# Cross-attention scores in two 64-row strips of the array, keys replicated through device memory, stages unrolled

## The chip, the cores and the metric

The kernel runs on one core of one Trainium2 chip. The metric is the device time of one execution in microseconds, the median of several runs. TensorE is called PE here, VectorE DVE, ScalarE ACT, GpSimd POOL, and SyncE (which issues all DMAs of this kernel) SP.

## What is computed

Four attention layers run one after the other on a small query block `x` (8 batches, 100 rows, width 128) against a long context `ctx` (8 batches, 1444 rows, width 128). All have 16 heads of 8 elements. Layers 0, 1 and 3 attend to the whole context. Layer 2 attends to its first 100 rows under a causal mask and has a feed-forward part.

```python
q, k, v = x @ Wq + bq, ctx @ Wk + bk, ctx @ Wv + bv     # 16 heads of 8
scores = einsum('bhqd,bhkd->bhqk', q, k) / sqrt(8)      # 16 x 100 x 1444 for each batch
attn = softmax(scores, axis=-1)
out = einsum('bhqk,bhkd->bhqd', attn, v)                # then projection, residual, norm
# layer 1: score = where(mask, -inf, score); the mask is all False in these inputs
```

## The kernel before

**Units and stages.** A unit is one batch of layer 0, 1 or 3: 24 units. Five steps of different units run side by side in a stage: `load` reads the context of a unit, `prep` transposes it and makes keys and queries, `top` makes the scores for the row maximum and the values, `exp` makes the scores again, takes the exponential and multiplies by the values, `post` normalises and projects. A unit moves on by one step per stage, so there are 24 stages with an `exp` unit, three ahead of them and one behind. Layer 2 of a batch rides along in the stages where layer 3 is loaded and prepared.

**Steps.** A stage has 48 steps (`NSTEP`): 12 chunks of 120 or 121 context rows, by 4 groups `t` of 4 heads. At step j every engine runs its part of `exp` tile j, and what the tables `AT` and `AT2` place at j: the transposes `ct0..2`, keys `k0..2`, queries `q`, values `v0..2`, and so on. Each of these is a few matmuls into one of two PSUM banks (`shared`), read by ACT or DVE. All engines run their instructions in the order in which they are written, and wait on semaphores whose names say what they count (`probs_ready` k: ACT has made k tiles of exponentials).

**A score tile.** Keys and queries are each split into two float16 parts, and the product is the sum of three: high by high, high by low, low by high. These three stand below each other in the rows of the array: 3 parts by 32 (4 heads of 8) are 96 rows (`PARTS`). The stationary operand is a piece of `krep` (96 rows, 120 context rows as columns), the moving operand `qmax` (96 rows, 4 heads by 100 queries = 400 columns, with zeros where the row is of another head). For `exp` the tile is `qexp`, a copy of `qmax` with a 97th row that holds minus the maximum, against a row of ones in `krep`. So at each step PE runs one matmul of 400 columns into one of two banks `sexp` (it waits until ACT has read the tile before the last), then one or two of 400 columns into one of three banks `smax`, which DVE folds into `mx`:

```python
MAX_AT = [i * 39 // NSTEP for i in range(NSTEP)]   # 48 maximum tiles in steps 0 to 38
def exp_scores(u, j, masks):      # PE, L700
    pe.wait_ge(*at(pe, "probs_ready", u, j - SR + 1))                      # SR = 2
    pe.matmul(ps, krep[:, u.par, t, c0:c0 + r], qexp[:, u.par, t, :, :]...)
def max_scores(u, j, masks):      # PE, L664
    pe.wait_ge(*at(pe, "smax_used", u, j - MR + 1))                        # MR = 3
    pe.matmul(ps, krep[0:PARTS, u.par, t, c0:c0 + r], qmax[:, u.par, t, :, :]...)
```

**Behind the scores.** ACT turns `sexp` into `probs` (L965). Every fourth step PE multiplies four tiles of `probs` by `vx` into `acc` (L719, 8 float32 matmuls, recorded as 16; each uses a strip of 32 columns of the array, four strips at a time). At step 39, when DVE has folded all 48 tiles, PE transposes `mx` into the banks `smax` (L676), DVE takes the maximum (`mneg`, L1102), PE transposes it at step 42 (L684), ACT copies it (`mrow`), and a DMA puts it into row 97 of `qexp` for the next stage.

**Keys.** ACT and POOL make `kp` (128 rows: 4 groups of 32; high and low part). `replicate` (SP, L403) spreads it into `krep` with 12 DMAs for each of the three groups of chunks, 36 a unit, of 30 KB each. ACT may overwrite `kp` for the next unit when these have landed.

**Loops.** `pipeline` writes most stages out, but stages 1 to 4, 9 to 12 and 17 to 20 as a hardware loop of two passes over two stages, whose semaphore counts stand in registers (`at`, L266). On PE, a branch on a flag computed from the mask stands ahead of stage 7: the variant of stages 7 to 15 that adds the mask is not taken with these inputs.

Of the kernel before, what the change touches and what calls it, by code (L numbers as in the profile page):

```python
# [21 lines left out]
F32 = mybir.dt.float32  # L22
# [9 lines left out]
KEYS = 1444  # L32
# [15 lines left out]
PARTS = 3 * 32  # L48
# [17 lines left out]
      "v0": 22, "v1": 24, "v2": 26, "mk0": 28, "mk1": 30, "mk2": 32, "mn": 42}  # L66
# [6 lines left out]
        "v1": 0, "v2": 1, "mk0": 0, "mk1": 1, "mk2": 0, "mn": 1, "flag": 1}  # L73
# [3 lines left out]
         "pt22": 1, "pt23": 0, "o2": 1, "mn": 0}  # L77
TOGETHER = 4
VALUES_AT = [j // TOGETHER * TOGETHER + TOGETHER + 1 for j in range(NSTEP)]
MAX_AT = [i * 39 // NSTEP for i in range(NSTEP)]  # L80
MT_AT = 39
# [3 lines left out]
class Unit:  # L85

    def __init__(self, layer, batch, reg=None, parity=None):
        self.L, self.batch, self.reg = layer, batch, reg
        self.par = batch % 2 if parity is None else parity

    def rows_of(self, tile):

        if self.reg is None:
            return tile[:, self.batch, :]
        return tile[:, bass.ds(self.reg + self.batch if self.batch else self.reg, 1), :].rearrange("s a d -> s (a d)")


def build(nc, ctx_in, x_in, mask_in, w_qkv, w_o, w_1, w_2, rows_in, cols_in, bq_in, headmask_in, heads_in, ident_in,
          causal_in, out):
    with ExitStack() as es:  # L100
# [3 lines left out]
        def psum(name, banks=1):  # L104
# [16 lines left out]
        headmask = sb("headmask", [PARTS, HT])  # L121
        headmask16 = sb("headmask16", [PARTS, HT], F16)
# [30 lines left out]
        krep = sb("krep", [PARTS + 1, 2, T, KEYS], F16)  # L153
# [5 lines left out]
        qmax = sb("qmax", [PARTS, 2, T, HT, S], F16)  # L159
        qexp = sb("qexp", [PARTS + 1, 2, T, HT, S], F16)  # L160
        mx = sb("mx", [128, T * QW], F16)
# [31 lines left out]

        smax = [psum(f"smax{i}") for i in range(MR)]
# [12 lines left out]
            "q_parts": one, "q_spread": one, "qexp_in": [16, 16, 0, 16], "v_filled": G, "v_ready": G,  # L207
# [3 lines left out]
            "m_ready": [2, 2, 0, 2], "mn_filled": one, "mrow_ready": one, "mrow_in": [16, 16, 0, 16],  # L211
# [9 lines left out]
        for g in range(3):  # L221
            PER[f"krep_in{g}"] = [16 * 12 * bool(n) for n in NG]

        for name, per in {"nat2_in": 32, "cx2_filled": 1, "cx2_read": 1, "kqv2_filled": 1, "kqv2_read": 1,
# [10 lines left out]
                "OT": ("oT_ready", 1), "wo": ("wo_read", 1), "cx2": ("cx2_read", 1), "kqv2": ("kqv2_read", 1),  # L235
# [10 lines left out]
        registers = {}  # L246

        def at(engine, name, u, k):


            per = PER[name][u.L]
            value = B * sum(PER[name][:u.L]) + per * u.batch + k
            if u.reg is None or not per:
                return sem[name], max(value, 0)
# [8 lines left out]
            if value == 0:  # L263
                return sem[name], term
# [1052 lines left out]
```

## Time and profile before

| | |
|---|---|
| time, median of 3 runs | 1240.93 us (1237.69 to 1241.09) |
| time of the profiled execution | 1242.44 us |
| its span, first to last instruction | 1240.6 us |
| mean granted clock of PE | 0.959 |
| busy: PE, DVE, ACT, POOL | 85%, 69%, 67%, 30% of the span |
| ahead of the first `exp` tile | 91.2 us |
| stages 0 to 7 (layer 0) | 357.9 us |
| `exp` stage 5; 17 (with layer 2); 23 (`exp` alone) | 40.8; 52.1; 30.4 us |

A matmul is recorded from its start until its modelled end, some 0.17 us after its last column has entered, so a busy PE isn't a full PE. "Idle before" is the time an engine stood still ahead of an instruction, with what ended it.

### The profile page before, as it was taken

How to read it: one execution, taken by the hardware profiler on the slowest of the kernel's cores; microseconds unless marked ns; L12 is line 12 of the kernel's file. 1: busy time of each engine (PE TensorE's matmuls, PEld its weight loads, DVE VectorE, ACT ScalarE, POOL GpSimd, SP SyncE). 2: the span in 40 equal slices, each digit the busy share in tenths (PEclk: the TensorE clock that was granted, in tenths of full speed). 3: DMA queues.
4: the chain of work that ended last, by engine and by line, in shares of the span. 5: the costliest groups of instructions: out<-in, count | busy, mean ns of one | idle time of the engine just before them, and what ended most of it. 6: DMA issues, size and time to landing. Idle time of an engine off the chain costs nothing.

```text
span 1240.6 us, 30123 instructions
## 1 busy us (share of the span) xinstructions
PE 1059.6 (85%) x9938; PEld 638.9 (51%) x9938; DVE 857.3 (69%) x1757; ACT 825.3 (67%) x1788; POOL 372.6 (30%) x339
## 2 busy tenths in 40 slices
PE   1469888888998999988998889998999989998886
PEld 0245445445555555655555555565556556565442
DVE  5678678578766766875876657576777858777650
ACT  1237756667776777776777676657677766767565
POOL 6744433344411311330231413232242413323000
PEclk9979999899999999998999999799999999999898
DMA  7212212212221221221232120202021121201100
GB/s 187 62 37 58 61 27 58 58 30 60 65 58 33 73 74 32 72 79 38 58 77 52 39 71 21 55 24 58 22 62 35 48 61 28 61 24 31 35 3 4
DMA packets 57587, 62.92 MB, mean 51 GB/s; under 512 B 16826, under 2 KB 50906, under 8 KB 57302
## 3 DMA queue, kind: packets, MB, share of 16 engines
q1 hardware_dynamic: 57430, 60.89, 19.0%
q8 instruction: 91, 1.49, 0.5%
q14 instruction: 66, 0.54, 0.1%
HBM read 23.63 MB, written 0.41 MB: 19 GB/s over the span
## 4 chain that ended last, share of the span: by engine, by line
PE 58%; DVE 16%; issue 10%; ACT 10%; SPq 3%; DMA 1%; POOL 1%; DVEq 0%; ACTq 0%; POOLq 0%
PE sexp L700 15%; PE acc L719 14%; PE smax L664 12%; DVE mx L1096 7%; ACT probs L965 5%; PE shared L616 3%; PE shared L604 3%; SPq L403 2%; DVE mneg L1102 2%; PE shared L593 2%; PE shared L784 2%; PE smax L676 1%; DVE qs L1083 1%; PE shared L626 1%; SPq L469 1%
## 5 line engine op out<-in xcount | busy, mean ns | idle before, releaser
L965 ACT ACTIVATE probs<-sexp 120x400 f32<-120x400 f32 (+1 forms) x1152 | 558.9, 511 | 237.9 <-PE sexp L700 226.6
L1096 DVE TENSOR_TENSOR mx<-smax,mx 120x400 f16<-120x400 f32 (+1 forms) x1056 | 557.2, 567 | 167.7 <-PE smax L664 161.4
L700 PE MATMUL sexp<-qexp,krep 97*120 97x400 f16 (+1 forms) x1152 | 403.8, 360 | 61.1 <-ACT probs L965 41.8
L664 PE MATMUL smax<-qmax,krep 96*120 96x400 f16 (+1 forms) x1152 | 367.3, 350 | 37.5 <-DVE mx L1096 29.1
L700 PEld LDWEIGHTS sexp<-qexp,krep 97*120 97x120 f16 (+1 forms) x1152 | 152.1, 136 | 216.7 <-ACT probs L965 144.6
L719 PE MATMUL acc<-probs,vx 120*18 120x200 f32 (+1 forms) x4608 | 262.1, 347 | 1.0 <-ACT probs L965 0.9
L664 PEld LDWEIGHTS smax<-qmax,krep 96*120 96x120 f16 (+1 forms) x1152 | 157.6, 138 | 92.6 <-DVE mx L1096 51.3
L488 POOL TENSOR_TENSOR ct<-ctf,ct 128x480 f16<-128x480 f32 (+1 forms) x72 | 82.8, 1151 | 346.2 <-ACT ct L902 346.2
L719 PEld LDWEIGHTS acc<-probs,vx 120*18 120x18 f32 (+1 forms) x4608 | 109.0, 99 | 114.8 <-issue 84.5
L1094 DVE CAST mx<-smax 121x400 f16<-121x400 f32 x96 | 51.3, 570 | 120.3 <-PE smax L664 120.2
L488 POOL TENSOR_TENSOR kp<-kf,kp 128x480 f16<-128x480 f32 (+1 forms) x72 | 79.2, 1106 | 114.6 <-ACT kp L916 114.6
L516 POOL TENSOR_TENSOR qmax<-qs,headmask 96x400 f16<-96x400 f16 x96 | 79.0, 852 | 52.9 <-DVE qs L1084 52.9
L494 POOL TENSOR_TENSOR rstd<-vare,half 100x1 f32<-100x1 f32 x24 | 13.0, 542 | 223.1 <-DVE vare L1113 223.1
L927 ACT COPY vx<-shared 120x512 f32<-120x512 f32 (+1 forms) x72 | 42.4, 589 | 50.7 <-PE shared L616 50.7
L604 PE MATMUL shared<-ct,wk 128*128 128x480 f16 (+1 forms) x216 | 60.4, 391 | 14.9 <-ACT kp L916 4.8
L593 PE MATMUL shared<-ident,nat 120*128 120x120 f32 (+1 forms) x288 | 46.9, 291 | 27.0 <-DMA causal<-in_causal 20.5
L1102 DVE TENSOR_REDUCE mneg<-smax 100x8 f16<-100x968 f16 x48 | 53.7, 1160 | 17.8 <-PE smax L676 17.8
L616 PEld LDWEIGHTS shared<-wv,ct 128*120 128x120 f16 (+1 forms) x864 | 62.1, 139 | 6.0 <-DVE sc L1166 1.8
L616 PE MATMUL shared<-wv,ct 128*120 128x128 f16 (+1 forms) x864 | 63.1, 225 | 1.1 <-DVE sc L1166 1.1
L593 PEld LDWEIGHTS shared<-ident,nat 120*128 120x128 f32 (+1 forms) x288 | 39.1, 156 | 34.1 <-DMA causal<-in_causal 20.5
L916 ACT ACTIVATE kf<-shared,cols 128x480 f32<-128x480 f32 (+1 forms) x48 | 32.0, 666 | 16.3 <-PE shared L604 15.1
L604 PEld LDWEIGHTS shared<-ct,wk 128*128 128x128 f16 x216 | 17.5, 99 | 43.3 <-issue 26.2
(133 smaller groups left out, 994.0 us busy)
## 6 DMA issues: line engine op xcount, KB each, us to landing
nat<-in_ctx SPq DMA_DIRECT2D x24, 720.0 KB
krep<-kp SPq DMA_DIRECT2D x576, 30.0 KB, 1.9
krep<-kp SPq DMA_DIRECT2D x288, 30.2 KB, 1.9
qexp<-qmax SPq DMA_DIRECT2D x24, 300.0 KB, 3.4
maskexp<-maskmax SPq DMA_DIRECT2D x8, 281.2 KB, 3.4
anymask<-in_mask SPq DMA_DIRECT2D x1, 1128.1 KB, 6.7
mask<-in_mask SPq DMA_DIRECT2D x8, 141.0 KB
wq<-in_w_qkv SPq DMA_DIRECT2D x1, 768.0 KB
```

The source lines that it names most:

```text
L488: pool.tensor_tensor(dst[:, 1, c0:c0 + n], src[:, c0:c0 + n], dst[:, 0, c0:c0 + n], ALU.subtract).then_inc(sem[done], 1)
L516: last = pool.tensor_tensor(qmax[:, u.par, t, :, :], qs[:, t, :].unsqueeze(1).broadcast_to([PARTS, HT, S]), headmask16[:, :].unsqueeze(2). ...
L593: last = pe.transpose(ps[:, to:to + r], nat[0:r, c, :], ident[0:r, 0:r])
L604: last = pe.matmul(ps[:, 0:n], wk16[:, w, u.L, :], ct[:, u.par, c, c0:c0 + n], start=(j == 0), stop=(j == 2))
L616: last = pe.matmul(ps[0:r, D * i:D * i + D], ct[:, u.par, p, c0:c0 + r], wv16[:, w, u.L, :], start=(j == 0), stop=(j == 2))
L664: last = pe.matmul(ps, krep[0:PARTS, u.par, t, c0:c0 + r], qmax[:, u.par, t, :, :].rearrange("p h s -> p (h s)"), start=True, stop=not masks)
L700: last = pe.matmul(ps, krep[:, u.par, t, c0:c0 + r], qexp[:, u.par, t, :, :].rearrange("p h s -> p (h s)"), start=True, stop=not masks)
L719: last = pe.matmul(acc[32 * q:32 * q + VW, 2 * S * slot:2 * S * slot + 2 * S], vx[0:r, u.par, PAIRS * c + 2 * t + p, :], probs[0:r, j % PR ...
L965: act.activation(probs[0:r, j % PR, :], sexp[j % SR][0:r, 0:QW], ACT.Exp).then_inc(sem["probs_ready"], 1)
L1094: op = dve.tensor_copy(dst, src)
L1096: op = dve.tensor_tensor(dst, src, dst, ALU.max)
L1102: dve.tensor_reduce(mneg[:, 8 * i:8 * i + 8], smax[i][0:S, :].bitcast(F16).rearrange("s (h n) -> s h n", h=8)[:, :, 0:chunk(0)[1]], AX, AL ...
```

## The change

Score products use half of the array's rows. A strip of 64 rows holds 2 heads: 3 parts by 16 rows (`KROWS` = 48), then a row for the maximum. Heads 4t and 4t+1 stand in the upper strip (rows 0 to 63), 4t+2 and 4t+3 in the lower one, so that one query tile `qx` (128 rows, 2 heads by 100 = 200 columns for each t) holds all four. Both uses read it: the maximum products rows 0 to 47 of a strip, the `exp` products 49 rows. It has three buffers; `qexp` and its DMA are gone. A tile of 400 columns is now one strip of two t, two matmuls of 200 columns each. The tile for `exp` and the tile for the maximum are taken in turn, and since `LEAD` is odd they always lie in different strips and different banks.

The 48 maximum tiles are spread one to a step, and run 13 tiles ahead (`LEAD`): the first 13 of a unit fall into steps 35 to 47 of the stage before. `mx` has two buffers, and its transposes go to the `shared` banks, at steps 36 and 37; `mn` is at 41.

Keys go to device memory first (`kept`, 3 DMAs a unit) and are read back into `krep` with 6 DMAs a group instead of 12, each 16 rows by 4 t. ACT may overwrite `kp` when the 3 writes have landed. All stages are written out, without loops or register counts.

```diff
-PARTS = 3 * 32
+PARTS = 128
+STRIP = 64
+KROWS = 48
-MAX_AT = [i * 39 // NSTEP for i in range(NSTEP)]
-MT_AT = 39
+LEAD = 13
+        kept = nc.dram_tensor("kept", (2, 128, 2, KEYS), F16, kind="Internal").ap()
-        def at(engine, name, u, k):
...
+        def at(name, u, k):
+
+            return sem[name], max(B * sum(PER[name][:u.L]) + PER[name][u.L] * u.batch + k, 0)
+        def tile_of(j):
+
+            return j // T, j // 2 % 2, j % 2
+        def max_tile(s, j):
+
+            u, i = (s.top, j + LEAD) if j + LEAD < NSTEP else (s.prep, j + LEAD - NSTEP)
+            return (u, i) if u is not None else None
-                b0 = units[n].batch if 0 <= n < len(units) else None
-                if b0 == 1 and n + 3 <= last:
...
-                    with engine.Fori(1, 4, 2) as b:
...
+                run(stage_of(n, units), n)
+                n += 1
-                for t in range(T):
+                for i in range(2):
                     for j, part in enumerate((0, 0, 1)):
-                        sp.dma_start(krep[32 * j:32 * j + 32, u.par, t, c0:c0 + n],
-                                     kp[32 * t:32 * t + 32, part, c0:c0 + n]).then_inc(sem[f"krep_in{g}"], 16)
+                        at_row = STRIP * i + 16 * j
+                        sp.dma_start(krep[at_row:at_row + 16, u.par, :, c0:c0 + n],
+                                     kept[u.par, :, part, c0:c0 + n].rearrange("(t i r) n -> i r t n", t=T, i=2)[i]
+                                     ).then_inc(sem[f"krep_in{g}"], 16)
+            def max_product(u, j, a, masks):
...
+                    pe.wait_ge(*at("smax_used", u, j - MR + 1))
+                at_row = STRIP * i
+                ps = smax[j % MR][0:r, 0:QW]
+                last = pe.matmul(ps[:, 2 * S * a:2 * S * a + 2 * S], krep[at_row:at_row + KROWS, u.par, 2 * tp + a, c0:c0 + r],
+                                 qx[at_row:at_row + KROWS, u.third, 2 * tp + a, :, :].rearrange("p f s -> p (f s)"),
...
+            def exp_product(u, j, a, masks):
...
+                    pe.wait_ge(*at("probs_ready", u, j - SR + 1))
+                at_row = STRIP * i
+                ps = sexp[j % SR][0:r, 0:QW]
...
-                    if s.exp is not None:
-                        exp_scores(s.exp, j, masks and s.exp.L == 1)
-                    for i in range(NSTEP):
-                        if MAX_AT[i] == j and s.top is not None:
-                            max_scores(s.top, i, masks and s.top.L == 1)
+                    m = max_tile(s, j)
+                    for a in range(2):
+                        if s.exp is not None:
+                            exp_product(s.exp, j, a, masks and s.exp.L == 1)
+                        if m is not None:
+                            max_product(*m, a, masks and m[0].L == 1)
```

The same place of PE's program before and after, in a stage of layer 0 around step 24, where `v1` lies. Before, steps 23 to 25; `sexp` and `smax` are score banks, `shared` the values, `acc` the products with the values:

```order
L700 MATMUL sexp1<-qexp,krep 120x400 [waits probs_ready]
L664 MATMUL smax2<-qmax,krep 120x400 [waits smax_used]
L700 MATMUL sexp0<-qexp,krep 120x400 [waits probs_ready]
L664 MATMUL smax0<-qmax,krep 120x400 [waits smax_used]
L616 MATMUL shared0<-wv16,ct 120x128 [waits q_read]
L616 MATMUL shared0<-wv16,ct 120x128 x11
L700 MATMUL sexp1<-qexp,krep 120x400 [waits probs_ready]
L664 MATMUL smax1<-qmax,krep 120x400 [waits smax_used]
L719 MATMUL acc<-probs,vx 18x200 x8
```

After, steps 24 and 25:

```order
L661 MATMUL sexp0<-qx,krep 120x200 [waits probs_ready]
L622 MATMUL smax1<-qx,krep 120x200 [waits smax_used]
L661 MATMUL sexp0<-qx,krep 120x200
L622 MATMUL smax1<-qx,krep 120x200
L572 MATMUL shared0<-wv16,ct 120x128 [waits q_read]
L572 MATMUL shared0<-wv16,ct 120x128 x11
L661 MATMUL sexp1<-qx,krep 120x200 [waits probs_ready]
L622 MATMUL smax2<-qx,krep 120x200 [waits smax_used]
L661 MATMUL sexp1<-qx,krep 120x200
L622 MATMUL smax2<-qx,krep 120x200
L683 MATMUL acc<-probs,vx 18x200 x8
```

Each pair of 400 columns became four of 200 that alternate; the second half of an `exp` tile now stands behind the wait for `smax_used`.

The end of a stage on PE, where the maxima are transposed (`mx`, then `mneg`). Before:

```order
L664 MATMUL smax2<-qmax,krep 120x400 [waits smax_used]
L700 MATMUL sexp1<-qexp,krep 120x400 [waits probs_ready]
L676 MATMUL smax0<-ident16,mx 100x121 [waits smax_used]
L676 MATMUL smax0<-ident16,mx 100x121 x7
L676 MATMUL smax1<-ident16,mx 100x121 x8
L700 MATMUL sexp0<-qexp,krep 120x400 [waits probs_ready]
L700 MATMUL sexp1<-qexp,krep 120x400 [waits probs_ready]
L719 MATMUL acc<-probs,vx 18x200 x8
L700 MATMUL sexp0<-qexp,krep 120x400 [waits probs_ready]
L684 MATMUL shared1<-ident16,mneg 16x100 [waits mask_ready,m_ready]
```

After:

```order
L661 MATMUL sexp0<-qx,krep 120x200 [waits probs_ready]
L622 MATMUL smax1<-qx,krep 121x200 [waits smax_used]
L661 MATMUL sexp0<-qx,krep 120x200
L622 MATMUL smax1<-qx,krep 121x200
L638 MATMUL shared1<-ident16,mx 100x121 [waits v_ready,smax_used]
L638 MATMUL shared1<-ident16,mx 100x121 x7
L661 MATMUL sexp1<-qx,krep 120x200 [waits probs_ready]
L622 MATMUL smax2<-qx,krep 121x200 [waits smax_used]
L661 MATMUL sexp1<-qx,krep 120x200
L622 MATMUL smax2<-qx,krep 121x200
L683 MATMUL acc<-probs,vx 18x200 x8
L638 MATMUL shared0<-ident16,mx 100x121 [waits v_ready,smax_used]
```

The transposes moved from `smax` to the `shared` banks, and the next unit's maximum tiles (121 rows: its first chunk) run on around them.

## Rows read from the trace of the kernel before

**Rows 1.** The page: the span, and busy time by engine.
```profile
span 1240.6 us, 30123 instructions
PE 1059.6 (85%) x9938; PEld 638.9 (51%) x9938; DVE 857.3 (69%) x1757; ACT 825.3 (67%) x1788; POOL 372.6 (30%) x339
```

**Rows 2.** The page: the chain that ended last, by engine.
```profile
PE 58%; DVE 16%; issue 10%; ACT 10%; SPq 3%; DMA 1%; POOL 1%; DVEq 0%; ACTq 0%; POOLq 0%
```

**Rows 3.** Stages 14, 5, 17 and 23: length, busy time by engine, PEclk, DMA share, GB/s.
```profile
728.50:787.20 58.70, 53.45 (x470) 32.72 (x469) 39.18 (x86) 38.32 (x84) 16.58 (x14) 0.89 0.17 45
318.40:359.20 40.80, 37.72 (x383) 22.17 (x382) 29.86 (x60) 30.70 (x68) 9.90 (x10) 1.00 0.22 55
899.40:951.50 52.10, 48.10 (x467) 30.49 (x467) 39.26 (x85) 37.72 (x84) 16.57 (x14) 1.00 0.18 46
1201.00:1231.40 30.40, 24.52 (x243) 10.14 (x242) 2.90 (x13) 21.79 (x49) 0.54 (x1) 1.00 0.01 3
```

**Rows 4.** Groups by line: busy us, mean ns, idle before.
```profile
L965 ACT ACTIVATE probs<-sexp 120x400 f32<-120x400 f32 (+1 forms) x1152 | 558.9, 511 | 237.9 <-PE sexp L700 226.6 <-issue 4.1
L1096 DVE TENSOR_TENSOR mx<-smax,mx 120x400 f16<-120x400 f32 (+1 forms) x1056 | 557.2, 567 | 167.7 <-PE smax L664 161.4
```

**Rows 5.** PE in order of time, steps 20 to 24 of stage 11: start, length.
```profile
602.84 0.50 PE L664 MATMUL smax<-qmax,krep 96*120 96x400 f16 x2
603.27 0.88 PE L719 MATMUL acc<-probs,vx 120*18 120x200 f32 x16
604.08 0.38 PE L700 MATMUL sexp<-qexp,krep 97*120 97x400 f16 x1
...
605.05 0.84 PE L616 MATMUL shared<-wv,ct 128*121 128x128 f16 x12
605.72 0.33 PE L700 MATMUL sexp<-qexp,krep 97*120 97x400 f16 x1
605.90 0.33 PE L664 MATMUL smax<-qmax,krep 96*120 96x400 f16 x1
606.07 0.33 PE L700 MATMUL sexp<-qexp,krep 97*120 97x400 f16 x1
```

**Rows 6.** ACT in order of time, late in stage 5, with maximum tiles.
```profile
346.00 2.05 ACT L965 ACTIVATE probs<-sexp 120x400 f32<-120x400 f32 x4 [0.78 <-PE sexp L700]
348.83 2.05 ACT L965 ACTIVATE probs<-sexp 120x400 f32<-120x400 f32 x4 [0.79 <-PE sexp L700]
```

**Rows 7.** ACT in order of time in stage 23, without maximum tiles.
```profile
1210.20 1.93 ACT L965 ACTIVATE probs<-sexp 121x400 f32<-121x400 f32 x4 [0.32 <-PE sexp L700]
1212.75 1.94 ACT L965 ACTIVATE probs<-sexp 120x400 f32<-120x400 f32 x4 [0.61 <-PE sexp L700]
```

**Rows 8.** The chain of stages 0 to 7 (91.2 to 449.1 us), by line.
```profile
by line: PE sexp L700 18.6%; PE acc L719 16.7%; PE smax L664 16.7%; issue 6.9%; DVE mx L1096 6.7%; PE shared L616 4.9%; ACT probs L965 4.9%; PE shared L604 4.6%; DVE mneg L1102 3.7%; PE shared L593 3.3%; DVE qs L1083 2.6%; DVE ssq L1063 1.6
```

**Rows 9.** Waits of the whole span: us in total, times, longest.
```profile
PEld smax L664 <- DVE mx L1096: 51.3, 82, 3.4
PEld smax L676 <- DVE mx L1096: 14.2, 16, 1.3
PEld shared L684 <- DVE mneg L1102: 6.6, 8, 1.7
```

**Rows 10.** PE's weight loads in order of time: behind two of four such gaps.
```profile
229.16 0.18 PEld L700 LDWEIGHTS sexp<-qexp,krep 97*121 97x121 f16 x1 [3.47 <-issue]
1005.85 0.13 PEld L700 LDWEIGHTS sexp<-qexp,krep 97*121 97x121 f16 x1 [3.51 <-issue]
```

**Rows 11.** The stretch around the first of them, columns as in rows 3.
```profile
228.10:234.70 6.60, 5.53 (x29) 3.20 (x30) 2.01 (x4) 2.67 (x6) 1.10 (x1) 0.50 0.18 46
```

**Rows 12.** PE in order of time: the first maximum tile.
```profile
44.86 0.92 PE L664 MATMUL smax<-qmax,krep 96*121 96x400 f16 x2 [6.53 <-POOL qmax L516]
```

**Rows 13.** The chain before stage 0: first key DMA's issue, last one's landing.
```profile
34.95 0.63 SPq L403
57.17 1.82 DMA krep<-kp
```

More of the change, by code:

```diff
@@ L320, in build @@
         held = [None, None]
-        def last_uses(s):
-            ends = [(AT["v1"], "v1", s.top), (AT["mk2"], "mk2", s.prep if s.prep.L == 1 else None),
-                    (AT["mn"], "mn", s.top), (AT2["o"], "o2", s.att2)]
-            for _, use, u in sorted((x for x in ends if x[2] is not None), key=lambda x: x[0]):
-                held[bank(use, u)] = (use, u)
         def await_read(pe, i):
@@ L393, in replicate @@
             def replicate(u, g, before, steps):
                 _, c0, n, _ = groups()[g]
-                counts = [at(sp, "k_lo", u, g + 1)]
+                sp.wait_ge(*at(f"k_kept{g}", u, 16))
                 if before is not None:
-                    counts.append(at(sp, "sexp_ready", before, steps))
-                for count in counts:
-                    sp.wait_ge(*count)
-                for t in range(T):
+                    sp.wait_ge(*at("sexp_ready", before, steps))
+                if u is UNITS[0] and g == 0:
+                    sp.wait_ge(sem["ones_ready"], 2)
@@ L869, in stage @@
                         queries(s.prep)
-                    if s.top is not None and j == MT_AT:
-                        maxima(s.top)
+                    for i in range(2):
+                        if s.top is not None and j == AT[f"mt{i}"]:
+                            maxima(s.top, i)
                     if s.top is not None and j == AT["mn"]:
@@ L1207, in stage @@
                 for j in range(NSTEP):
-                    for i in range(NSTEP):
-                        if MAX_AT[i] == j and s.top is not None:
-                            maximum(s.top, i)
+                    m = max_tile(s, j)
+                    if m is not None:
+                        maximum(*m)
                     if s.post is not None and j == AT["O"] + 1:
@@ L1226, in stage @@
                             power(s.load, part)
-                    if s.top is not None and j == MT_AT:
-                        for i in range(2):
+                    for i in range(2):
+                        if s.top is not None and j == AT[f"mt{i}"]:
                             maxima(s.top, i)
@@ L1272, in _ @@
             dve.memset(ones[:, :], 1.0).then_inc(sem["rest_ready"], 1)
[L1273 removed]
+            pipeline(UNITS, stage, first=-2)
 def kernel(**inputs):
```

447 lines of the change are left out of this document (204 added, 243 removed).

## Prediction

> **What bounds the kernel now.** I read the page first. No engine is full: PE is recorded busy for 85% of the span, DVE for 69%, ACT for 67%, POOL for 30% [rows 1]. PE's share is of matmuls whose recorded ends overlap, so the chain says more: it runs through PE for 58%, through DVE for 16%, through ACT for 10% [rows 2]. The table by stage shows the same balance in a stage without layer 2: 40.8 us long, ACT busy 30.7, DVE 29.9 [rows 3]. Neither could carry the stage alone, and a stage could not be much shorter than 31 us however fast PE was.
>
> PE in order of time gives the true price of its work. With nothing to wait for, score matmuls of 400 columns start 0.17 us apart (605.72, 605.90, 606.07), and twelve matmuls of 128 columns with as many weight loads start (0.84 - 0.22) / 11 = 0.056 us apart [rows 5]. A group of `acc` takes from 603.27 to 604.08. The two score tiles of each of 48 steps are thus 48 x 0.34 = 16.3 us of each stage, its largest item.
>
> How much of that stands on the path is seen in two ways. Bare steps, without preparation: four tiles of exponentials take 348.83 - 346.00 = 2.83 us with maximum tiles beside them [rows 6], and 1212.75 - 1210.20 = 2.55 us in the last stage, which has none [rows 7]. So four maximum tiles, 0.68 us of PE, cost 0.28 us there. ACT's four tiles are 1.94 us of this; the rest is the wait behind `acc`. In steps with preparation PE is the tighter one: the chain of the eight stages of layer 0 runs through L664 for 16.7% of 357.9 us, 59.8 us, or 7.5 us a stage [rows 8].
>
> **The change, part by part.**
>
> *Two strips side by side.* A step has four matmuls of 200 columns in place of two of 400. If the strips work at once, a step's scores take 0.17 us instead of 0.34, 8.2 us less PE time a stage. Of this the path gives back between 0.28 x 39/4 = 2.7 us (maximum tiles now stand in 39 of 48 steps, all priced as bare) and 7.5 us (all of L664 on the chain). Both kinds of step fill a stage about equally, so I take the middle, 5.1 us, for the 23 stages that have maximum tiles: **-118** (bounds -62 and -172). ACT's and DVE's tiles keep their shapes and counts (511 and 567 ns each [rows 4]).
>
> The trace has no two row strips at work, but it has four column strips: the 16 `acc` records start within 0.88 - 0.33 = 0.55 us, 0.037 us apart for 200 float32 columns, where the 400-column float16 ones need 0.17 [rows 5]. That makes overlap likely for rows too. The Trainium skill, "TensorE: Matmul & The Clock Gate", part 3, says that matmuls in different row groups run concurrently, starting about 4 ns apart; the trace before cannot confirm that.
>
> *Weight loads.* There are four of 120 columns a step instead of two. At 0.056 us each one behind the other they are 0.22 us, more than the 0.17 of the matmuls. If they don't overlap between strips, a stage gains 0.05 x 48 = 2.4 us less; with PE's 58% of the path that is +32 over 23 stages. I take 0 and keep it for the range.
>
> *Turns between modes.* Score tiles now use 64-row strips, the preparation the whole array, `acc` column strips. The trace has the last turn: the score matmul at 602.84 + 0.50 - 0.33 = 603.01 has let in its columns by 603.18, and `acc` starts at 603.27: 0.09 us. The way back: the last `acc` matmul starts at 603.82, is in by 603.99, and `sexp` starts at 604.08, 0.09 again [rows 5]. Between scores and preparation there was nothing: 605.72 follows the values at matmul pace. There are 17 such places in a stage of layer 0, 4 of them behind `acc` already, so 30 new turns; 36 with the mask's transposes; some 56 with layer 2. In all (30 + 36 + 56) x 8 = 976 turns, 88 us of PE. After a turn to the preparation ACT or DVE waits for its result; the turn back lies under their copy of it. I take half: **+44** (bounds 0 and +88). The Trainium skill, "TensorEngine Tiling (Array Packing)", Key Properties, says that changing the tiling mode drains the engine; this speaks against the change, and the 0.09 us above agrees with it. By the rule all 976 turns would count, +88.
>
> *Maxima.* Before, PE stopped at step 39 for DVE's last tile, and at 42 for `mneg`: 14.2 and 6.6 us in all [rows 9]. With the last tile at step 34, transposes at 36 and 37 into other banks and `mn` at 41, other tiles lie between: **-21**. The work itself is the same.
>
> *Loops.* Four gaps of PE of 3.5 to 3.9 us are put down to "issue" at a stage's start; those at 229.16 and 1005.85 are back edges [rows 10], and so is one at 580.78. They go: **-11**. The fourth, at 404.05, is the branch on the mask flag, and stays, one stage earlier. Stages that are already written out show no such gap, so I cost the longer program at 0.
>
> *Keys.* SP's issues of 0.63 us [rows 13], 36 a unit, are 22.7 us; now there are 18 with twice the pieces, and 3 writes. In the loop of stages the copy may begin at exp step 16 and is needed at step 35, some 16 us later, against six issues of perhaps 1 us and two landings of 1.8 [rows 13]: hidden. If it weren't, PE would stop at step 35. Before stage 0 it matters: ACT waited for the last landing at 57.17 + 1.82 = 59.0 before the next unit's keys, and maximum tiles, which began at 44.86 [rows 12], were then held behind the next unit's transposes. Thirteen of them now come first: **-5**.
>
> *Queries.* POOL spreads half the columns, and one copy by DMA goes; DVE's split of the queries works on 128 rows instead of 96 with as many columns. All this has steps to spare, priced at 0.
>
> *A new wait.* The second half of an `exp` tile stands behind the maximum's wait for DVE. Behind it are ACT's next tile and `acc`. PE waited there 51.3 us in 82 waits [rows 9]; ACT has one more tile to work on, (2.05 - 0.51) / 3 = 0.51 us at most and 0.45 at its best, so some 51.3 - 82 x 0.45 = **+14** get through (bounds 0 and +51).
>
> The sum: -118 + 44 - 21 - 11 - 5 + 14 = -97. The profiled execution took 1242.4 us, its span 1240.6 plus 1.8 around it, and lies 1.5 above the median of the runs. 1242.4 - 97 - 1.5 = **1144 us**.
>
> **The rivals.**
>
> - *PE drops off the path.* The gain is -172, the turns cost nothing, the new wait 14: 1242 - 172 - 21 - 16 + 14 = 1047 at best, 1080 with part of the turns. For it: 7.5 us on L664's chain. Against: ACT's chain is close behind in bare steps. Chance 0.15.
> - *Turns and loads eat the gain.* Lower bound of the gain, all turns, serial loads: -62 + 88 + 32 - 21 - 16 + 14 = +35; with half of the loads and three quarters of the turns, 1240. It needs PE to be the tight engine at the turns but not in the scores, which [rows 6] and [rows 7] allow for bare steps only. As a band of 1200 to 1245: chance 0.16.
> - *The strips don't overlap* (the change doesn't do what it says). Scores keep 0.34 us a step, and the turns are paid three quarters: 0 + 66 - 21 - 16 + 14 = +43, 1284. Slower. Against it are the column strips in [rows 5]. Chance 0.09.
> - *The clock falls.* PE is granted half speed in stretches behind its gaps: 0.50 from 228.1 to 234.7, around the gap that ends at 229.16 [rows 10, 11]. Stage 14 at a mean of 0.89 took 58.7 us where stage 17, with the same work and a clock of 1.00, took 52.1 [rows 3]: 6.6 us for 0.11 x 58.7 x 2 = 12.9 us at half speed, 0.51 per us. PE's array now has 8 us less work in each stage, and might be judged idle oftener. The gain of 97 is gone at 190 us more of half speed, a mean clock of 0.88 instead of 0.96; at 0.80 the kernel takes some 1320. Slower. Chance 0.10.
> - *Late keys* through device memory, or other waits that leave no change: chance 0.03.
>
> The forecast itself has 0.47, with a range of its own from 1090 to 1200.
>
> **How the numbers follow.** From the forecast and the first rival the time lies from 1050 to 1200 with 0.62; the range reaches up over the second rival to 1240 and down to 1065, and leaves out the two slower ones. About 0.3%, 4 us, is what a measurement of this kernel can tell from no change. Faster: 0.47 + 0.15 + 0.13 of the second rival = 0.75; within 0.3%: 0.04; slower: 0.09 + 0.10 + 0.02 = 0.21.
>
> **What would show it.** Strips: in the new trace score matmuls of neighbouring steps start in pairs a few ns apart, four of them in 0.17 us. Weight loads: L661 and L622 loads starting closer than 0.05 us. Turns: 0.09 us of idle array on both sides of each preparation. Bare steps: four tiles of ACT in 2.55 to 2.65 us. Maxima: no wait of L638 for DVE. Loops: one gap of over 3 us on PE, not four. New wait: ACT's waits for L661 that end with DVE's tile. I'd be wrong if the pairs start 0.08 us apart or more, if the mean clock is under 0.9, or if ACT's wait for `sexp` (226.6 us [rows 4]) grows.

## The result

The changed kernel takes **1310.5 us** (median of four runs, 1297.1 to 1319.5) against 1241.0 (1237.7 to 1242.7) of the kernel before, run beside it: 1.053 times as long, 95% interval 1.045 to 1.061. It is slower; 1144 was forecast. Medians here and below are of all runs of a kernel, and ratios leave out a run that is over 1.5% above its kernel's shortest, here the one of 1319.5.

The page of the profile after, which answers to [rows 1] and [rows 2], with the granted clock in 40 slices:

```profile
span 1309.2 us, 30985 instructions
PE 1144.4 (87%) x12242; PEld 671.1 (51%) x12242; DVE 868.2 (66%) x1758; ACT 831.9 (64%) x1788; POOL 339.9 (26%) x339
PEclk9999977877978788889687779887788977779675
PE 63%; DVE 13%; ACT 12%; issue 8%; SPq 1%; DMA 1%; POOL 1%; ACTq 0%; POOLq 0%; DVEq 0%
```

PE is recorded busier than before and its share of the chain grew from 58% to 63%. The mean granted clock is 0.829 in place of 0.959. PE is granted one of two clocks, 2.4 or 1.2 GHz. A mean of 0.829 thus says that 1309.2 x (1 - 0.829) x 2 = 448 us of the span were at 1.2, against 102 before.

Stages 4, 14, 17 and 23 after, in the columns of [rows 3]:

```profile
274.00:325.30 51.30, 46.72 (x480) 26.36 (x480) 33.64 (x64) 31.21 (x68) 16.91 (x16) 0.70 0.21 52
762.20:820.30 58.10, 52.08 (x566) 31.03 (x567) 39.59 (x87) 38.59 (x85) 15.22 (x14) 0.88 0.20 53
940.10:997.90 57.80, 55.31 (x563) 32.80 (x564) 39.00 (x86) 38.76 (x84) 15.29 (x14) 0.80 0.19 49
1257.80:1299.90 42.10, 34.68 (x290) 15.70 (x289) 2.89 (x13) 21.87 (x49) 0.54 (x1) 0.53 0.01 3
```

Stage 17 had the full clock before and took 52.1 us; now it has 0.80 and takes 57.8. Stage 23, which has no maximum tiles and no preparation, went from 30.4 us at 1.00 to 42.1 at 0.53. DVE's and ACT's own work is the same size. Their waits for PE grew instead (groups as in [rows 4]):

```profile
L1062 DVE TENSOR_TENSOR mx<-smax,mx 120x400 f16<-120x400 f32 (+1 forms) x1056 | 570.7, 570 | 324.9 <-PE smax L622 319.4
L931 ACT ACTIVATE probs<-sexp 120x400 f32<-120x400 f32 (+1 forms) x1152 | 556.5, 512 | 307.7 <-PE sexp L661 295.9
```

ACT waited 295.9 us for `sexp` (226.6 before), DVE 319.4 for `smax` (161.4).

Yet the mechanism itself works. PE in order of time, at full clock in stage 11 (columns as in [rows 5]):

```profile
608.80 0.29 PE L661 MATMUL sexp<-qx,krep 49*121 49x200 f16 x1
608.80 0.29 PE L622 MATMUL smax<-qx,krep 48*120 48x200 f16 x1
608.93 0.25 PE L661 MATMUL sexp<-qx,krep 49*121 49x200 f16 x1
608.94 0.25 PE L622 MATMUL smax<-qx,krep 48*120 48x200 f16 x1
609.11 0.88 PE L683 MATMUL acc<-probs,vx 121*18 121x200 f32 x16
609.92 0.29 PE L661 MATMUL sexp<-qx,krep 49*121 49x200 f16 x1
```

The two strips start in the same hundredth of a microsecond. Bare steps are what was forecast, too: ACT's four tiles at the end of stage 11 take 641.22 - 638.67 = 2.55 us (2.83 in [rows 6]):

```profile
638.67 1.93 ACT L931 ACTIVATE probs<-sexp 120x400 f32<-120x400 f32 x4
641.22 0.90 ACT L931 ACTIVATE probs<-sexp 120x400 f32<-120x400 f32 x2 [0.61 <-PE sexp L661]
```

Of the four gaps of PE of over 3 us one is left, the branch on the mask flag:

```profile
367.73 0.18 PEld L661 LDWEIGHTS sexp<-qx,krep 49*121 49x121 f16 x1 [3.82 <-issue]
```

So the question is which of two theories holds. **Clock**: half-empty columns of the array, 48 or 49 rows of 128, bring the clock down, and that alone is the loss. **Turns**: the turns between tiling modes and the doubled loads eat the gain and more, and the clock only follows the gaps that they make.

### The profile page after: what moved, and what is told of

Read it like the earlier page. It is cut to its first block, busy times and chain, and to the rows that moved or that the text cites. A ratio compares the mean times of both kernels' runs of the same rounds, so it can differ in the third digit from the quotient of the medians.

```text
span 1309.2 us, 30985 instructions
## 1 busy us (share of the span) xinstructions
PE 1144.4 (87%) x12242; PEld 671.1 (51%) x12242; DVE 868.2 (66%) x1758; ACT 831.9 (64%) x1788; POOL 339.9 (26%) x339
## 4 chain that ended last, share of the span: by engine, by line
PE 63%; DVE 13%; ACT 12%; issue 8%; SPq 1%; DMA 1%; POOL 1%; ACTq 0%; POOLq 0%; DVEq 0%
PE sexp L661 18%; PE acc L683 17%; ACT probs L931 7%; DVE mx L1062 4%; PE smax L622 4%; PE shared L560 4%; PE shared L549 4%; PE shared L572 3%; PE shared L638 3%; PE shared L748 2%; ACT kp L882 2%; PE shared L582 2%; PE shared L738 1%; DVE qs L1049 1%; PE shared L729 1%
## 5 line engine op out<-in xcount | busy, mean ns | idle before, releaser
L1062 DVE TENSOR_TENSOR mx<-smax,mx 120x400 f16<-120x400 f32 (+1 forms) x1056 | 570.7, 570 | 324.9 <-PE smax L622 319.4
L931 ACT ACTIVATE probs<-sexp 120x400 f32<-120x400 f32 (+1 forms) x1152 | 556.5, 512 | 307.7 <-PE sexp L661 295.9
L661 PE MATMUL sexp<-qx,krep 49*120 49x200 f16 (+1 forms) x2304 | 454.5, 303 | 74.2 <-ACT probs L931 67.0
L622 PE MATMUL smax<-qx,krep 48*120 48x200 f16 (+1 forms) x2304 | 450.7, 304 | 20.3 <-DVE mx L1062 12.3
L661 PEld LDWEIGHTS sexp<-qx,krep 49*120 49x120 f16 (+1 forms) x2304 | 245.1, 150 | 304.0 <-ACT probs L931 187.6
L683 PE MATMUL acc<-probs,vx 120*18 120x200 f32 (+1 forms) x4608 | 317.5, 404 | 1.7 <-ACT probs L931 1.0
L622 PEld LDWEIGHTS smax<-qx,krep 48*120 48x120 f16 (+1 forms) x2304 | 242.5, 152 | 39.7 <-DVE mx L1062 27.5
L549 PE MATMUL shared<-ident,nat 120*128 120x120 f32 (+1 forms) x288 | 63.3, 362 | 23.4 <-POOL nat L492 21.5
L1068 DVE TENSOR_REDUCE mneg<-shared 100x8 f16<-100x968 f16 x48 | 55.9, 1164 | 22.6 <-PE shared L638 22.6
L472 POOL TENSOR_TENSOR qx<-qs,headmask 128x200 f16<-128x200 f16 x96 | 47.1, 522 | 53.6 <-DVE qs L1050 53.6
L638 PE MATMUL shared<-ident,mx 121*100 121x121 f16 x384 | 40.0, 266 | 1.0
```

Of the source, the lines that this page charges most:

```text
L549: last = pe.transpose(ps[:, to:to + r], nat[0:r, c, :], ident[0:r, 0:r])
L622: last = pe.matmul(ps[:, 2 * S * a:2 * S * a + 2 * S], krep[at_row:at_row + KROWS, u.par, 2 * tp + a, c0:c0 + r], qx[at_row:at_row + KROWS ...
L638: last = pe.transpose(ps[0:S, :].bitcast(F16)[:, 128 * h:128 * h + n], mx[0:n, u.par, col:col + S], ident16[0:n, 0:n])
L661: last = pe.matmul(ps[:, 2 * S * a:2 * S * a + 2 * S], krep[at_row:at_row + KROWS + 1, u.par, 2 * tp + a, c0:c0 + r], qx[at_row:at_row + K ...
L683: last = pe.matmul(acc[32 * q:32 * q + VW, 2 * S * tp:2 * S * tp + 2 * S], vx[0:r, u.par, PAIRS * c + 2 * (2 * tp + a) + i, :], probs[0:r, ...
L931: act.activation(probs[0:r, j % PR, :], sexp[j % SR][0:r, 0:QW], ACT.Exp).then_inc(sem["probs_ready"], 1)
```

## The experiments

All medians are of four runs, each beside runs of the kernel before (1240.4 to 1244.0). Clocks are those of the profiled runs. The edits are shown shortened, with a word or a comment in place of what is left out.

### Rows without any other change

The changed kernel with both uses over all 64 rows of a strip. Queries are zero in the added rows, so no score changes; instructions, columns and turns are the same.

```diff
-krep[at_row:at_row + KROWS, ...], qx[at_row:at_row + KROWS, ...]            # L622
-krep[at_row:at_row + KROWS + 1, ...], qx[at_row:at_row + KROWS + 1, ...]    # L661
+krep[at_row:at_row + STRIP, ...], qx[at_row:at_row + STRIP, ...]            # both
```

> Both uses multiply all 64 rows of a strip instead of 48 or 49; the added rows hold zeros in the queries. No cost in columns. If rows in use keep the clock up: clock 0.86 to 0.90 and 1270 to 1295 us. If not, or if zeros don't count: 1300 to 1320 us as the changed kernel.

Measured: **1230.1 us**, ratio to before 0.990 (0.985 to 0.994), clock 0.91. Rows that multiply zeros took 80 us off, twice the most that the expectation allowed. Stage 3, and stage 10 of layer 1, now have the full clock throughout:

```profile
220.00:260.70 40.70, 35.19 (x480) 20.50 (x481) 33.47 (x65) 30.68 (x69) 16.93 (x16) 1.00 0.24 66
509.90:550.80 40.90, 37.24 (x491) 22.99 (x491) 32.50 (x69) 32.83 (x72) 9.13 (x11) 1.00 0.28 76
```

This gives the price of the clock without a theory. Stage 4 of the changed kernel has the work of stage 3 here: 51.3 us with 51.3 x 0.30 x 2 = 30.8 at half speed, against 40.7 with none, 0.34 us for each us at half speed. The whole kernels give (1310.5 - 1230.1) / (448 - 221) = 0.35. It is a price for this kernel, where ACT and DVE set part of the pace; it isn't the same in every stage. Stage 23, 30.4 us at 1.00 and 42.1 at 0.53, gives 0.30.

The same kernel with real query values in the added rows, against ones in the keys:

```diff
-np.concatenate([parts] * 3 + [np.zeros_like(parts)], axis=-2)
+np.concatenate([parts] * 4, axis=-2)          # and headmask is set on those rows too
```

> The 64-row kernel, but the added rows 49 to 63 hold real query values instead of zeros, against ones in the keys; each score is moved by an amount that is the same for all keys, which the softmax takes out again. If rows in use count, whatever they hold: 1230 at 0.91, as with zeros. If non-zero products count: a higher clock than 0.91 and under 1220. If more switching costs power and lowers the clock: over 1240.

**1226.2 us** at 0.915. What the rows hold makes no difference that can be told here.

The kernel before, with its score products over 128 rows instead of 96 and 97. Beside some fills ahead of the first stage nothing else is changed:

```diff
-krep = sb("krep", [PARTS + 1, 2, T, KEYS], F16)
+krep = sb("krep", [128, 2, T, KEYS], F16)      # qmax, qexp alike, zero below row 97
```

> The kernel before, with the score products over 128 rows instead of 96 and 97: the added rows hold zeros in the queries and ones in the keys; no instruction is added to a stage. If the rows that a matmul uses keep the clock up, zeros or not, the stretches at half speed of stages 13 to 16 (55 to 58.7 us) shrink to about 53 us each, so some 1225 us at a clock of 0.975 or more. Rival: the clock depends on the data's products or on busy time alone: 1241 at 0.959, no change.

**1226.1 us**, ratio 0.987 (0.981 to 0.993), clock 0.976, where the rows theory had 1225 at 0.975. More rows, at no cost in instructions, help the old kernel as well.

### Strips not abreast, and a filler

Both tiles of a step in the same strip:

```diff
-LEAD = 13
+LEAD = 12
```

> LEAD 12 instead of 13: both tiles of a step lie in the same strip, so nothing runs side by side and PE streams as many columns one after the other as before, over half the rows. Theory A in the form that the time the array streams counts: clock 0.93 or more, 1225 to 1250 us. Theory A in the form that rows in use count: clock stays near 0.83 or lower, 1330 us or more, as the scores are serial too. Theory B: as the changed kernel plus up to 8 us of PE a stage, 1310 to 1400 us.

**1547.1 us**, ratio 1.242 (1.233 to 1.252), clock 0.721. The four score matmuls now stand one behind the other:

```profile
380.99 0.29 PE L661 MATMUL sexp<-qx,krep 49*120 49x200 f16 x1
381.12 0.25 PE L622 MATMUL smax<-qx,krep 48*120 48x200 f16 x1
381.21 0.25 PE L661 MATMUL sexp<-qx,krep 49*120 49x200 f16 x1
381.30 0.25 PE L622 MATMUL smax<-qx,krep 48*120 48x200 f16 x1
```

PE streams the scores' columns for twice as long and is recorded busy for 91% of the span, and the clock is the lowest of all runs: over 48 rows, streaming time alone doesn't keep it up. Of the three cases in the expectation only the one with rows, 1330 us or more, holds the time. Why the clock fell even below 0.829 isn't shown.

The 64-row kernel with one more matmul of 400 columns over a strip in each step, overwritten by the scores:

```diff
+pe.matmul(smax[j % MR][0:r, 0:QW], krep[64 rows of the strip], qx[64 rows, 400 columns], start=True, stop=True)
```

> As the 64-row kernel, and one more matmul of 400 columns a step whose product is overwritten, ahead of the step's scores: 8 us more streaming a stage, in time in which PE mostly waits. Theory A: clock 0.93 or more, and in spite of the added work 1200 to 1250 us. Theory B: 1310 us or more.

**1276.2 us** at 0.934. The clock rose from 0.91, as expected, but the time is over the 1250 that went with it. Stage 3, at full clock, takes 42.5 us instead of 40.7, and the total is 46 us worse:

```profile
224.00:266.50 42.50, 38.86 (x528) 24.61 (x527) 33.46 (x65) 30.77 (x69) 16.92 (x16) 1.00 0.24 63
```

Here idle work was a poor way to buy the clock; rows in matmuls that run anyway cost no time.

### Everything but the strips

One matmul of 400 columns over all 128 rows for a tile of 4 heads. `qx` is 4 heads wide, with zeros where the row is of another head; lead, keys through device memory, banks and written-out stages are those of the changed kernel.

```diff
-qx = sb("qx", [PARTS, 3, T, 2, S], F16)
+qx = sb("qx", [PARTS, 3, T, HT, S], F16)
-two matmuls of 200 columns: krep[at_row:at_row + KROWS, ...], qx[at_row:at_row + KROWS, ...]
+last = pe.matmul(ps, krep[:, u.par, t, c0:c0 + r], qx[:, u.third, t, :, :].rearrange("p f s -> p (f s)"), ...)
```

> One matmul of 400 columns over all 128 rows for each score tile, in place of two of 200 in a strip; lead, banks, keys through device memory and unrolled stages as in the changed kernel. Theory A (the half-speed clock of PE, 0.83 on average against 0.96, is what costs, and it fell because the strips use less of the array): clock back to 0.93 or more and 1190 to 1220 us, under the kernel before. Theory B (the lead, the keys or the new waits cost, and the clock only follows the waits): clock stays under 0.88 and 1280 us or more.

**1268.7 us** at 0.956: the clock that was expected if the strips had brought it down, but 49 us over the time. This run carried a cost of its own: the row of the maximum was written by eight DMAs in place of two, and PE waited for the last at each stage's start (waits of that kernel: us in total, times, longest):

```profile
PEld sexp L660 <- DMA qx<-mrow: 71.9, 24, 3.8
```

With two DMAs (the heads of a strip stored next to each other in `qx`):

```diff
-qx = sb("qx", [PARTS, 3, T, HT, S], F16)
+qx = sb("qx", [PARTS, 3, HT, T, S], F16)
```

> As the first full-array kernel (one matmul of 400 columns over 128 rows for a tile, lead, keys through device memory and written-out stages as in the changed kernel), but the maximum's row is written by two DMAs instead of eight. If the eight DMAs were what stopped PE at each stage's end (3.4 us, 24 times there, 2.9 of it beyond what the changed kernel waits), it takes 1268.7 - 24 x 2.9 = some 1199 us at the same clock of about 0.95, faster than before, and then the strips alone cost 1310.5 - 1199 = 111 us. Rival: the full array itself is slow here (its scores take twice the time on PE); then it stays above 1240.

**1176.7 us**, ratio 0.946 (0.941 to 0.952), clock 0.984. It beats both kernels, and its clock is down in hardly any slice:

```profile
PEclk9989999999999999999999999999899999999999
212.80:254.00 41.20, 38.31 (x384) 21.60 (x383) 33.50 (x65) 30.41 (x69) 18.27 (x16) 1.00 0.25 65
585.10:626.30 41.20, 39.44 (x396) 24.11 (x395) 32.92 (x69) 32.57 (x73) 10.51 (x11) 1.00 0.30 77
683.00:736.90 53.90, 47.85 (x471) 30.07 (x470) 39.88 (x87) 38.33 (x85) 16.63 (x14) 1.00 0.23 57
1139.00:1169.50 30.50, 24.52 (x243) 10.04 (x242) 2.90 (x13) 21.94 (x49) 0.54 (x1) 1.00 0.01 3
```

(The first line is of the page; the others are stages 3, 12, 14 and 23.) The strips thus cost 1310.5 - 1176.7 = 134 us, against some 111 expected. And a second surprise: at full clock a stage takes 41.2 us with the whole array and 40.7 to 40.9 with strips. Of the 60 us that strips, turns and new wait were to bring, at full clock too only some 0.4 x 24 = 10 are there. (The 0.4 is read in layers 0 and 1; no stage with layer 2 ran at full clock in strips.)

Strips of 64 rows for units 0 to 12 and the whole array for units 13 to 23:

```diff
+self.full = self.number >= 13      # u.full: one matmul over 128 rows; else two in a strip
```

> Strips with all 64 rows (as in the 64-row kernel) for units 0 to 12, one matmul over the full array for units 13 to 23, where layer 2 rides along. From the stage tables: the 64-row kernel's stages 0 to 12, 41.9 us each on average, and the full-array kernel's stages 13 to 23 less 2.9 us each, some 39 us less in sum than the 64-row kernel's: 1230 - 39 = 1191, clock 0.94. Rival: the clock falls in layer 2's stages for layer 2's own reasons and not for the rows of the scores; then it takes 1220 to 1230.

**1212.9 us** at 0.970, worse than the whole array throughout, and between the two expectations, 1191 and 1220 to 1230. Stages 13 to 23, in which layer 2 rides along, answer the rival that their clock falls for layer 2's own reasons. This kernel, with the whole array there, and below it the 64-row kernel:

```profile
659.50:1201.20 541.70, 480.94 (x4706) 291.34 (x4704) 380.24 (x814) 384.65 (x842) 144.75 (x125) 0.99 0.18 47
636.20:1221.40 585.20, 519.58 (x5698) 305.08 (x5698) 373.10 (x814) 388.35 (x841) 132.35 (x125) 0.86 0.16 44
```

With the same work of layer 2 the clock is 0.99 and not 0.86: it is the scores in strips that bring it down there too. What was lost lies elsewhere. Where both kinds meet, in stage 12, PE turns ahead of and behind each full tile. That stage took 63.9 us, at a mean clock of 0.81. From its timeline, in a stretch at full clock:

```profile
601.50 0.29 PE L679 MATMUL sexp<-qx,krep 64*121 64x200 f16 x1
601.72 0.38 PE L626 MATMUL smax<-qx,krep 128*120 128x400 f16 x1
602.03 0.29 PE L679 MATMUL sexp<-qx,krep 64*121 64x200 f16 x1
602.26 0.63 PE L551 MATMUL shared<-ident,nat 120*128 120x120 f32 x4
```

A strip of 200 columns that needs 0.09 us (380.99's neighbours above) is followed after 0.22, and a full tile of 0.17 after 0.31: 0.13 to 0.14 us for each turn.

### Where the gain at full clock went

Three kernels split it. The first takes the scores' time away without strips: each matmul computes 200 of its 400 columns.

```diff
-qx[:, u.third, :, t, :]
+qx[:, u.third, 0:2, t, :]      # units 1 to 23; the other half of the tile keeps old numbers
```

> The full-array kernel, but each score matmul of the units after the first computes only 200 of its 400 columns (the other half of a tile keeps old numbers, so the output isn't the reference's): the scores' time on PE falls as much as with two strips abreast, without strips, turns or a second weight load. ACT and DVE work as before. If 5.1 us of the 8.2 that PE saves in a stage come off the path, as the prediction has it, stages at full clock fall from 41.15 to 36 us. Rival: the steps are set by other waits (ACT's exponentials behind acc, DVE, the preparation's chain) and give back 1.5 us or less at full clock. The clock may fall, since the array works less: 1065 us if it stays at 0.98 and the first holds, 1150 to 1250 if the second holds.

**1155.5 us** at 0.931. Stages 3 and 12, at full clock:

```profile
206.60:245.80 39.20, 31.95 (x386) 19.88 (x384) 33.09 (x66) 30.08 (x69) 18.27 (x16) 1.00 0.27 68
558.80:597.40 38.60, 33.64 (x397) 22.19 (x395) 32.67 (x69) 32.21 (x72) 10.51 (x11) 1.00 0.32 82
```

8.2 us less of PE in a stage bring 41.2 - 39.2 = 2.0 and 41.2 - 38.6 = 2.6 us, not 5.1. And without any strips the clock falls from 0.984 to 0.931 when the scores stream for half the time: to nearly what 64-row strips have, 0.91. Rows times columns are the same in both, 128 by 200 and 64 by 400 for a tile.

The second cuts each of these in two, so that loads and alternation are those of the strips, without turns:

```diff
+for a in range(2):      # exp, maximum, exp, maximum; 100 columns each
```

> The half-width full-array kernel (its output isn't the reference's, as there), with each score tile cut into two matmuls of 100 columns that alternate like the strips' (exp, maximum, exp, maximum): the same PE time for the scores as with two strips abreast, the same four weight loads, the same wait ahead of the second half of an exp tile, but no turns between tiling modes. Stages 2 and 12 at full clock took 39.14 and 38.61 us with two matmuls a step and 40.65 and 40.90 with strips. If the loads and the alternation take the 1.5 to 2.3 us back, they come out at 40.6 and 40.9 here; if it is the turns (0.10 us into and 0.13 us out of each preparation, by the timeline), they stay at 39.1 and 38.6.

**1185.9 us** at 0.92. Stages 4 and 12:

```profile
256.20:296.00 39.80, 33.58 (x480) 23.99 (x479) 33.21 (x64) 30.37 (x68) 18.28 (x16) 1.00 0.27 67
576.00:615.50 39.50, 35.55 (x492) 26.39 (x491) 32.82 (x68) 32.57 (x72) 10.52 (x11) 1.00 0.31 77
```

The same split at full width:

> The full-array kernel with each score tile in two matmuls of 200 columns that alternate in the same way: twice the weight loads and the second-half wait, at full width and without turns. If loads hide behind matmuls of 200 columns, 1176.7 us and 41.15 and 41.21 us in stages 2 and 12, as with two; if a load of 0.056 us each counts, up to 5.4 us a stage more, some 1250.

**1193.7 us** at 0.991, stages 3 and 12 at 41.80 and 42.00 us, 0.6 and 0.8 more than in one piece:

```profile
214.10:255.90 41.80, 38.58 (x482) 27.96 (x480) 33.53 (x65) 30.72 (x69) 18.30 (x16) 1.00 0.25 64
591.10:633.10 42.00, 40.06 (x493) 30.22 (x492) 32.99 (x68) 32.76 (x72) 10.54 (x11) 1.00 0.31 76
```

The expectation of the half-width split asked whether the loads or the turns take the gain back; both do. In a stage of layer 0 and in one of layer 1, at full clock:

| | layer 0 | layer 1 |
|---|---|---|
| shorter scores (41.2 to 39.2; 41.2 to 38.6) | -2.0 | -2.6 |
| four loads, alternation (to 39.8; 39.5) | +0.6 | +0.9 |
| the rest: turns (to 40.7; 40.9, the 64-row strips) | +0.9 | +1.4 |
| strips against the whole array | -0.5 | -0.3 |

How the middle is shared out is approximate, since two strips abreast have their loads beside each other and 100-column matmuls don't. The turns can be seen directly. The 64-row kernel around the values `v0`:

```profile
528.51 0.25 PE L661 MATMUL sexp<-qx,krep 64*120 64x200 f16 x1
528.51 0.25 PE L622 MATMUL smax<-qx,krep 64*120 64x200 f16 x1
528.69 0.89 PE L572 MATMUL shared<-wv,ct 128*121 128x128 f16 x12
529.50 0.29 PE L661 MATMUL sexp<-qx,krep 64*120 64x200 f16 x1
```

The half-width kernel at the same place:

```profile
499.46 0.25 PE L623 MATMUL smax<-qx,krep 128*120 128x200 f16 x1
499.54 0.84 PE L573 MATMUL shared<-wv,ct 128*121 128x128 f16 x12
500.22 0.25 PE L661 MATMUL sexp<-qx,krep 128*120 128x200 f16 x1
```

In strips the values start 0.18 us behind the last scores, here 0.08; the next scores come after 0.81, here 0.68. A preparation costs 0.10 + 0.13 = 0.23 us of PE in turns. These rows agree with "TensorEngine Tiling (Array Packing)", Key Properties, in the Trainium skill, by which changing the mode drains the engine: the way there adds 0.10 us and the way back 0.13.

The last pair has added turns: a tiny matmul over the full array ahead of each step's scores, in the 64-row kernel and in the whole-array kernel.

```diff
+pe.matmul(smax[j % MR][0:r, 0:8], krep[:, u.par, 0, c0:c0 + r], ident16[:, 0:8], start=True, stop=True)
```

> The 64-row kernel with one tiny matmul (8 columns, all 128 rows, overwritten by the scores behind it) ahead of the scores of each step that has a maximum tile: it adds two turns between tiling modes to a step, 96 a stage, and almost no streaming. Read in stages at full clock (40.65 us without it), against the pair with the same tiny matmul in the full-array kernel. If a turn costs 0.09 us of PE and PE is on the path, this stage grows by up to 96 x 0.09 = 8.6 us more than that of the pair; if turns are free or hidden, by as much as the pair's. Whole time, with what the clock then does: 1300 us in the first case, 1240 in the second.

> The full-array kernel with the same tiny matmul in each step; here it adds no turn, since the scores use the full array too. A stage at full clock (41.15 us without it) grows by the tiny matmul and its weight load alone, 48 x 0.056 = 2.7 us at most; whole time 1176.7 to 1240.

**1321.9 us** at 0.882 with strips, **1212.1 us** at 0.987 without. Stages 3 and 12 with strips:

```profile
233.60:275.70 42.10, 39.83 (x527) 25.54 (x527) 33.33 (x64) 31.62 (x68) 16.94 (x16) 1.00 0.26 64
642.70:686.10 43.40, 42.13 (x540) 28.04 (x540) 32.35 (x69) 33.81 (x73) 9.12 (x11) 1.00 0.29 73
```

And with the whole array:

```profile
214.80:257.00 42.20, 39.57 (x433) 24.99 (x432) 33.39 (x65) 30.84 (x69) 18.28 (x16) 1.00 0.25 63
598.70:641.40 42.70, 41.42 (x445) 27.42 (x444) 32.91 (x69) 33.10 (x73) 10.51 (x11) 1.00 0.30 75
```

Strips lose 42.1 - 40.7 = 1.4 and 43.4 - 40.9 = 2.5 us a stage, the whole array 1.0 and 1.5, within the 2.7 expected. For the strips the expectation counted 96 more turns a stage, but there are fewer: in stages 3 and 12 the tiny matmul stands behind a preparation in 17 and 20 of the 48 steps, where it adds no turn, and behind `acc` in 8, where it adds one. That makes 54 and 48, or 4.9 and 4.3 us at the expectation's 0.09, and they cost 0.4 and 1.0. PE's recorded busy time in stage 3 grew by 39.83 - 35.19 = 4.6 us and the stage by 1.4, so most of the added time lies where PE stood idle before. Yet the whole run is 92 us longer than without the tiny matmul, and over both times that were expected. The strips' clock fell from 0.91 to 0.882, (1322.1 x 0.118 - 1230.6 x 0.09) x 2 = 91 us more at half speed, some 31 at 0.34; with 24 x 2 = 48 at full clock that makes 79 of the 92. The other 13 aren't accounted for. Turns, then, do bring the clock down a little; they don't bring it to 0.829.

### Loops

```diff
-                if b0 == 1 and n + 3 <= last:
+                if False:
```

> The kernel before with all its stages written out and nothing else changed. The prediction's term: three gaps of 3.5 to 3.9 us go, -11 us, 1230. Rival: longer straight code costs as much in fetching instructions, no change; or the gaps that go also take stretches of half clock with them, then 1215 to 1225.

**1227.1 us**, ratio 0.989 (0.983 to 0.995), clock 0.968: -14, three more than the gaps. The clock is up from 0.959, which can be the three.

## Why the prediction was wrong

**The step that failed** is the clock: the sum has no term for it. The base is the old kernel's time at its 0.959, and the terms are added to it as if the new kernel would keep that clock. The rival *the clock falls* had 0.10, with the remark that the array "might be judged idle oftener". The runs show 448 us at half speed in place of 102, at 0.34 each **+118 us**. Without the clock's term the measured ones give 1241 - 42 - 10 = 1189 (worked out below), which lies inside the range of 1065 to 1240.

The remark was part of the reason. With the scores' PE time halved over the whole array the clock goes from 0.984 to 0.931. The other part is rows, which the prediction didn't count: the same scores went from 96 and 97 rows to 48 and 49. With rows alone raised to 64 the clock goes from 0.829 to 0.91, and the old kernel's, raised to 128, from 0.959 to 0.976.

That the rival's time for a clock of 0.80, some 1320, is close to 1310.5 at 0.829 is luck: its price of 0.51 us for a us at half speed was too dear (0.34 measured), and the 1144 under it too low (1189). The price came from stages 14 and 17, taken as equal work; in the old kernel over 128 rows both have the full clock and take 53.7 and 52.1 us, so that (58.7 - 53.7) / 12.9 = 0.39 would have been nearer. Two of the three things that were to prove the prediction wrong are there, a mean clock under 0.9 and a longer wait of ACT for `sexp`; the third, pairs 0.08 us apart, is not.

**Strips side by side, -118.** The mechanism was right (pairs in the same 0.01 us, bare steps 2.55 us), the size was the second thing that was wrong: -2.0 to -2.6 us a stage, not -5.1, some -46 to -60 in 23 stages. That is a little less even than the smaller bound, -62. The larger bound took all of L664 on the chain for time that would be given back; but the chain names whatever was last, and ACT and DVE stand close behind it.

**Turns, +44.** A turn to the preparation and back is 0.23 us, not 0.18, and shows as +0.9 to +1.4 us a stage, 22 to 34 us in all; 44 was somewhat too much. That a turn's price depends on its place is borne out by the added ones, and by the mixed kernel's stage 12, where PE is busy throughout and the stage took 63.9 us.

**Weight loads 0, new wait +14.** Together at most +0.6 to +0.9 us a stage, 14 to 22 us. Right in size.

**Maxima -21, loops -11, keys -5.** The whole-array kernel has these and no strips: 1176.7 - 1241 = -64. It also has 64 us less at half speed, -22 at 0.34, so -42 is left against -37 forecast. That the two are close is in part luck. Loops alone are -14. Of PE's waits for the maxima, 20.8 us before, the new transposes (L638) keep 8.1, so that these give 12.7 at most and not 21. Some 15 us are assigned to no part. That not all of the gain is clock can be read in stage 12, which had the full clock before, too, and took 41.20 us with the whole array:

```profile
627.00:670.80 43.80, 40.19 (x396) 24.81 (x397) 32.50 (x68) 32.96 (x74) 10.45 (x11) 1.00 0.25 63
```

The keys' -5 did not come: the changed kernel's stage 0 starts at 92.0 us, where it was 91.2. Late keys, the last rival, don't appear: no wait for `krep` is among those of over 2.5 us.

**The sum in measured terms.** -42 for what surrounds the strips, -10 for strips, loads and turns at full clock, and (448 - 102) x 0.34 = +118 for the clock: 1241 + 66 = 1307, measured 1310.5. The price 0.34 comes from a stage of this kernel, so this is a check that the parts fit and not a second proof. The same terms, with 38 us at half speed in the whole-array kernel, give (221 - 38) x 0.34 - 10 = 52 us between the 64-row and the whole-array kernel, where 1230.1 - 1176.7 = 53 were measured. The theory that the turns alone do it falls, since the 64-row kernel has every turn and is 80 us faster. That fewer rows lower the clock is shown, with all else the same. Why they do, and how rows, streaming time and turns add up, is not. Rows don't explain every stage either. Stage 23 of the 64-row kernel, and of its version with the filler, which has none of it there and so the same instructions:

```profile
1184.40:1221.40 37.00, 29.25 (x290) 13.63 (x290) 2.90 (x13) 21.97 (x49) 0.54 (x1) 0.71 0.01 2
1221.50:1263.60 42.10, 34.67 (x290) 15.70 (x289) 2.90 (x13) 21.88 (x49) 0.54 (x1) 0.53 0.01 3
```

The second has the 0.53 that the 48-row kernel has.

## What to carry to other kernels

Count rows as well as time: strips that leave out the zeros halve the rows in use for the same scores, and here the clock fell whether they ran abreast (0.829) or one behind the other (0.721). Where a kernel's clock already has dips, try to fill the contraction with zero rows, which cost no instruction, before removing PE work; it took some 14 us off the old kernel. Before paying for a faster PE, shorten its work artificially (half the columns) and read a stage at full clock, and the mean clock of the whole: here that would have shown 2.0 to 2.6 us a stage instead of 5.1, and a clock of 0.931 instead of 0.984.

## What had not been expected of the hardware

The granted clock did not follow recorded busy time. In the changed kernel PE is busy for 87% of the span at 0.829; the kernel before has 85% at 0.959; 48-row strips one behind the other have 91% at 0.721. With the same instructions 64-row strips have 0.91, with zeros or with values in the added rows. Kernels whose score tiles are 400 columns over 128 rows have 0.956 to 0.991. Rows aren't all of it: with 200 columns over the same 128 rows it is 0.931. The Trainium skill, "TensorE: Matmul & The Clock Gate", Part 1, describes the gate as following how busy PE has been; these runs show that how busy PE is recorded does not tell the clock by itself, and that rows which multiply zeros raise it. While the clock is full, the number of rows changes no time that shows: a 64-row and a 48-row strip both start their second matmul 0.13 us behind the first.
